# TensorE's expert steps 8 to 63 written out one by one instead of in two loops (adaLN block: attention and top-8 mixture of experts, one core)

## What is computed

```
logits = x @ router_weight.T
topw, topi = top_k(softmax(logits), 8);  topw /= sum(topw)
xe[e, c] = the rows of x that go to expert e, in order, 128 at most
g, u = split(xe @ gate_up_proj)          # per expert 128 x 256 @ 256 x 192
ye   = (silu(g) * u) @ down_proj         # per expert 128 x 96 @ 96 x 256
y[t] = sum over its experts of topw * ye
x = x + gb * y
```

## Time and profile before

| what | us |
|---|---|
| median of the runs (lowest to highest) | 299.39 (294.73 to 299.65) |
| the profiled execution, its own time | 296.88 |
| its span in the trace | 295.1 |
| TensorE matmuls, busy | 264.7 |
| VectorE, busy | 214.7 |
| ScalarE, busy | 157.2 |
| GpSimd, busy | 157.5 |

### The profile page before, as it was taken

How to read it: one execution, slowest core, us unless ns; L and a number is a source line. 1 busy time by engine, 2 the same in 40 slices (tenths; PEclk the granted TensorE clock), 3 DMA queues, 4 the chain that set the end, 5 groups by cost and what they waited for, 6 DMA issues and landing times.

```text
span 295.1 us, 6906 instructions
## 1 busy us (share of the span) xinstructions
PE 264.7 (90%) x2077; PEld 198.0 (67%) x2077; DVE 214.7 (73%) x658; ACT 157.2 (53%) x466; POOL 157.5 (53%) x156
## 2 busy tenths in 40 slices
PE   7878999998999899798766779999999999999991
PEld 2344677566766577466533468887888888879990
DVE  4397677878788986882452166899988988997386
ACT  4458498536863397345523256665666666642000
POOL 3723000003646455577677777688878888887000
PEclk9999999999999999999995999999999999999997
DMA  7999599999999914997394558999998999766933
GB/s 243 343 340 333 148 343 366 363 229 258 288 266 274 273 65 129 309 353 236 119 340 168 160 145 193 258 226 163 157 159 156 160 159 168 103 65 82 315 137 116
DMA packets 62123, 64.23 MB, mean 218 GB/s; under 512 B 5069, under 2 KB 57618, under 8 KB 62096
## 3 DMA queue, kind: packets, MB, share of 16 engines
q1 hardware_dynamic: 51664, 49.06, 58.3%
q0 software_dynamic: 10272, 14.85, 26.0%
q10 hardware_dynamic: 160, 0.01, 0.0%
HBM read 35.93 MB, written 28.45 MB: 218 GB/s over the span
## 4 chain that ended last, share of the span: by engine, by line
PE 45%; DVE 15%; DMA 13%; issue 9%; POOL 9%; ACT 7%; SPq 1%; ACTq 0%; DVEq 0%; POOLq 0%
PE bank L1295 8%; PE bank L1309 5%; POOL slot_rows L644 5%; DMA sum<-stage 4%; PE bank L962 4%; PE bank L1286 3%; DVE rmax L1459 2%; PE bank L974 2%; POOL sum L669 2%; PE bank L1038 2%; PE bank L1036 2%; PE bank L1068 2%; DMA arena<-sum 2%; PE bank L1022 2%; PE bank L993 2%
## 5 line engine op out<-in xcount | busy, mean ns | idle before, releaser
L635 POOL DMA_INDIRECT slot_rows<-stage x48 | 48.1, 1001 | 30.1 <-issue 6.1
L1295 PE MATMUL bank<-arena,stage 128*128 (+1 forms) x256 | 53.1, 329 | 0.0
L669 POOL DMA_INDIRECT sum<-kz,stage x24 | 37.2, 1552 | 10.2 <-issue 5.3
L1295 PEld LDWEIGHTS bank<-arena,stage 128*128 128x128 f32 x256 | 40.3, 190 | 1.0 <-issue 0.4
L1309 PE MATMUL bank<-arena,stage 96*128 (+1 forms) x128 | 38.9, 386 | 0.0
L891 ACT ACTIVATE stage<-bank 128x256 f32<-128x256 f32 x64 | 24.5, 383 | 22.5 <-PE bank L1286 22.1
L1459 DVE TENSOR_REDUCE rmax<-bank 128x2 f32<-128x512 f32 (+1 forms) x48 | 30.6, 684 | 4.8 <-PE bank L993 4.4
L669 POOL DMA_INDIRECT sum<-stage x16 | 25.5, 1594 | 5.9 <-issue 2.7
L1286 PE MATMUL bank<-cst,stage 128*128 128x128 f32 x128 | 25.1, 277 | 3.8 <-DMA stage<-slot_rows 3.0
L898 ACT ACTIVATE stage<-bank 128x96 f32<-128x96 f32 x64 | 16.0, 250 | 18.8 <-PE bank L1295 17.9
L1286 PEld LDWEIGHTS bank<-cst,stage 128*128 128x128 f32 x128 | 17.1, 141 | 13.2 <-DMA stage<-slot_rows 4.5
(11 more groups left out here) (214 smaller groups left out, 632.0 us busy)
## 6 DMA issues: line engine op xcount, KB each, us to landing
slot_rows<-zero_row SPq DMA_DIRECT2D x8, 1040.0 KB, 12.5
stage<-slot_rows SPq DMA_DIRECT2D x64, 130.0 KB
arena<-in_gate_up SPq DMA_DIRECT2D x10, 768.0 KB, 11.9
arena<-in_down SPq DMA_DIRECT2D x5, 768.0 KB, 12.4
sum<-zero_row SPq DMA_DIRECT2D x3, 1152.0 KB, 13.2
arena<-sum SPq DMA_DIRECT2D x12, 256.0 KB, 5.9
arena<-in_gate_up SPq DMA_DIRECT2D x2, 864.0 KB
arena<-in_wmod SPq DMA_DIRECT2D x1, 1024.0 KB, 6.2
```

Source lines behind the costliest of these rows:

```text
L635: pool.indirect_dma_start(slot_rows, bass.IndirectOffsetOnAxis(ap=idx[:, t, k:k + 1], axis=0), src[:, t, :], None, bounds_check=last_slot, ...
L669: pool.indirect_dma_start(sums[a], where, ye_ring[i % RING], None, compute_op=ALU.add).then_inc(added[a], 16)
L1295: last = mm(bank[2 + q % 2][:, 0:GU + 1], xeT[:, q % 2, k * CAP:(k + 1) * CAP], expert_w[:, s - 1, k * (GU + 1):(k + 1) * (GU + 1)], start ...
```

## The change

TensorE's two loops become plain sequences of steps. The steps themselves, their order, the six waits between the loops and all other engines' programs are the same. The group number and the step number are now constants, so the waits have constant values and the weights constant places.

```diff
             for j in range(GRP):
                 expert_steps(0, j, True, False)
-            with pe.Fori(1, EARLY // GRP) as i:
-                for j in range(GRP):
-                    expert_steps(i, j, False, False)
+            for s in range(GRP, EARLY):
+                expert_steps(s // GRP, s % GRP, False, False)
             pe.wait_ge(v_rcol, HC)
             for n in range(4):
                 pe.wait_ge(s_lw[n], 16 * 3)
             pe.wait_ge(s_lw[4], 16 * 3 * (AFTER_RESIDUAL - AFTER_O))
-            with pe.Fori(EARLY // GRP, E // GRP) as i:
-                for j in range(GRP):
-                    expert_steps(i, j, False, False)
+            for s in range(EARLY, E):
+                expert_steps(s // GRP, s % GRP, False, False)
             for j in range(3):
                 expert_steps(E // GRP, j, False, True)
```

## The result

The changed kernel takes 300.41 us (median of 22 runs, 297.72 to 302.74), the kernel before 297.38 us (22 runs, 294.73 to 300.17). The ratio is 1.0091 with a 95% interval of 1.006 to 1.0123: it is slower, by some 2.7 us. The ratio is that of the fast runs alone (two of the changed kernel's 22 fell in the chip's slower state), so it is not the quotient of the two medians. The forecast was no change.

A forecast was written before the change was run, and what follows sets the result against it. It took POOL, its DMAs, the loads of the sums and VectorE to bound the kernel. The sum was 296.88 - 0 + 0 = 296.9 us profiled, 299.4 around the median, taken as 299.0, range 295.2 to 302.0 us.

The forecast's parts named there:

- What bounds the stage: Expert stage: POOL, its DMAs, the loads of the sums and VectorE set the end; TensorE has 9.5 us of slack.
- rival A: Expert stage: POOL follows TensorE after all, so the gain arrives and the end is 1.8 us sooner, 297.2; chance 0.11.
- The loop's own cost: TensorE's loop boundaries: removing them gains between 1.2 and 2.25 us at step 64, taken as 1.8.
- The 2.3 us of slack at the end: Late products: TensorE's last matmul ends at 288.60, VectorE comes to what it needs at 290.90.
- Register work inside the steps: TensorE's steps: constants replace computed values, worth nothing, or at most 0.3 us over 56 steps.
- The packets: Instruction queues: some 4 packets more for the written-out program, each 1.2 us of one DMA engine.
- the product 4.7 x 5 / 46 = 0.5: POOL's adds: full packet cost of 4.7 us, scaled by some five tight adds of 46, gives 0.5 us.
- My own upper bound: POOL's adds: 4 x 1.2 = 4.7 us if each packet sat in front of an add that the next waits for.
- Four packets among thousands: DMA engines: argument against rival B that the few added packets are little beside all others; no size given.
- the 3.8 us that the kernel before loses among its adds: POOL's 46 adds: 88.98 us where 85.2 would do, lost to landings; also bounds what luckier DMA order could give.
- Rival B: DMA engines while the adds run: fetch packets slow POOL, 3 us, 302.0; sign: 46 adds over 91 us; chance 0.10.
- The spread: Whole kernel: the sum around the runs' median gives 299.4, lowered to 299.0 for the four executions shown.

The follow-up runs named there:

- the halves: Two kernels with only steps 8 to 31, or only steps 32 to 63, written out, against the kernel before: 1.0032 and 0.9988.
- `paused`: The changed kernel with three idle matmuls on TensorE ahead of each of the seven groups of eight: 1.0041 of the kernel before.
- `one_trip`: All seven groups of eight written out, each inside a loop of one trip, against the kernel before: 1.0019, and 1.0069 on another chip.
- the four sums: Kernel before and changed kernel, each with four sums in place of three, the fourth not loaded: 294.22 and 294.66 us.

## Why the prediction was wrong

- **What bounds the stage: right.** POOL, its DMAs, the loads of the sums and VectorE set the end. TensorE's gain did not arrive, and rival A is out: the last add starts 14.7 us after expert 59's output.
- **The loop's own cost: right in kind, too small.** I took 1.8 us, bounded by 2.25. It was 3.0. The bound held that TensorE's wait for VectorE between steps 21 and 24 (0.9 us) stays and takes gains back; after the change those steps cost 0.3 us over the pace. The 2.3 us of slack at the end was right too: TensorE now has to wait there.
- **Register work inside the steps: right, nothing.** 1.42 us before and after.
- **The packets: right in number, wrong in what they do to POOL.** I estimated four and there are three. I priced one at 1.2 us of one engine; those in the held flights take 0.9 to 1.7. The step that failed is the product 4.7 x 5 / 46 = 0.5, from which I took 0. It takes a packet to fall on a random add and to cost only where that add was tight already, and it takes only the held adds for tight. But an add with the median landing has some 0.1 us to spare, so a packet can make a held add where none was: the 46 adds take 2.4 us more with three packets more. About half of the packets did it, by 1.2 to 1.7 us, the others hardly. My own upper bound, now 3 x 1.2 = 3.6 us, was nearer than the product. That it comes to 0.8 us per packet is an average, and the halves, with 90.6 and 91.1 us for one or two packets more, don't follow it.
- **The evidence that I set against it was of the wrong kind.** "Four packets among thousands" counts packets of 1 KB against one of 16 KB. And the 3.8 us that the kernel before loses among its adds (3.9, as 46 x 1.85 is 85.1 and not 85.2; 3.1 are holds, the rest adds that took longer) were read as a stock of luck, when each hold was a place to ask what lay in its flight: the one at 221.50 us had a packet of each instruction queue in it, the one at 188.45 none.
- **Rival B fits best**: its place, the DMA engines while the adds run, and its price (3 us, measured 2.7). Its sign came true as well, with the 46 adds over 91 us and more idle time before them. It had a chance of 0.10. The range held the median, for B was in it, but the forecast of no change within 1.5 us was wrong.
- **The spread.** I moved the median down to 299.0 for the runs shown. 22 runs have 297.38 for the kernel before, so that was right in direction.

What stays open: how much of the 2.6 us is TensorE's earlier pace moving the slot loads. `paused` beside `one_trip` allows up to 1 us for it. That the loss goes through the landings is shown by the four sums. That packets in flight are its cause is read from the profiles of two kernels, and no run adds the packets without also changing TensorE's program or pace. Why the halves have slow adds with so few packets, and whether `one_trip` differs between two chips, stays open too.

## What to carry to other kernels

Writing a loop out trades its boundaries for program to fetch, and the fetch goes through the DMA engines (here 3.0 us less on TensorE for three packets of 16 KB). Where another engine waits for DMA landings with less spare time than one instruction packet takes, count the packets and put the time of each, in full, into the range of the forecast. Look first at what lies in the flights that are already held.

## What the runs showed that was not expected

- A loop of a single trip costs almost nothing at its boundary: `one_trip` has the 46 adds and TensorE's pace of the written-out kernel, where a loop of three or four trips took 0.25 to 0.5 us per group of eight. With a single trip the group's number is a constant as well, so this does not separate the branch from the register work.
- Eight semaphore clears in a step of 1.42 us stop TensorE from hiding its instruction issue: 24.8 us of its weight loads' waits have no releaser, in 55 places, and none in the changed kernel without them.
- An add to a sum in DRAM lands in 3.7 us at best and 6.0 at worst, median 4.7, in the 16 adds for which the first profile of the changed kernel gives it. With three sums and one add in 1.85 us that is the whole difference between a chain that never waits and one that loses 3 to 6 us.
